# Twenty instead of twelve weight buffers for the streamed experts of a two-layer macaron block, eight of them filled when the expert stage begins

## The reference, cut to what matters

```python
# x: 2048 tokens x 256, E = 64 experts, M = 176, C = 96 slots for each expert, 6 experts for each token
slot = flat * C + jnp.minimum(pos, C - 1)
buf = jnp.zeros((E * C, H)).at[slot].set(x[tok]).reshape(E, C, H)
g = jnp.einsum('ech,emh->ecm', buf, Wg)
u = jnp.einsum('ech,emh->ecm', buf, Wu)
out = jnp.einsum('ecm,ehm->ech', silu(g) * u, Wd).reshape(E * C, H)
y = jnp.sum(out[slot].reshape(T, K, H) * topk_w[..., None], axis=1)
```

## Time and profile before

| | |
|---|---|
| median of 3 runs | 1694.56 us (1693.66 to 1703.97) |
| profiled execution, span from first to last instruction | 1695.7 us |
| busy: PE / DVE / ACT / POOL | 85% / 63% / 44% / 46% |
| DMA traffic in all | 145.50 MB |
| expert stage of layer 0 in the span | 123.1 to about 296 us |
| expert stage of layer 1 in the span | 785.0 to about 950 us |

### The profile page before, as it was taken

How to read it: one execution, slowest core, us unless ns; L and a number is a source line. 1 busy time by engine, 2 the same in 40 slices (tenths; PEclk the granted TensorE clock), 3 DMA queues, 4 the chain that set the end, 5 groups by cost and what they waited for, 6 DMA issues and landing times. The chain is left out here.

```text
span 1695.7 us, 39494 instructions
## 1 busy us (share of the span) xinstructions
PE 1441.4 (85%) x14334; PEld 990.9 (58%) x14334; DVE 1075.4 (63%) x2743; ACT 750.3 (44%) x1786; POOL 773.8 (46%) x741
## 2 busy tenths in 40 slices
PE   6879999448889996888999478877899999998799
PEld 3556656414545554455566356654677777777687
DVE  6852222457876564783222388876998888874888
ACT  5533333254555633553333311125776666752322
POOL 4453332763320000454333466606998888973000
PEclk9989999569999998899999788888999999999899
DMA  8309995631110002514999232200000000000000
GB/s 265 98 14 267 284 266 150 204 96 38 38 38 1 1 1 67 152 40 123 280 296 259 73 87 84 78 4 13 3 16 3 12 7 3 16 3 3 10 19 22
DMA packets 92664, 145.50 MB, mean 86 GB/s; under 512 B 25032, under 2 KB 52528, under 8 KB 92512
## 3 DMA queue, kind: packets, MB, share of 16 engines
q1 hardware_dynamic: 62816, 93.06, 19.1%
q0 software_dynamic: 15360, 37.77, 7.7%
q10 hardware_dynamic: 14336, 12.59, 2.7%
HBM read 122.39 MB, written 18.87 MB: 83 GB/s over the span
## 5 line engine op out<-in xcount | busy, mean ns | idle before, releaser
L2298 POOL TENSOR_TENSOR sb_m_prob<-sb_m_prob,sb_m_rinv 128x512 f32<-128x512 f32 x256 | 260.1, 1041 | 44.6 <-DVE sb_m_rinv L2348 40.8
L1272 POOL DMA_INDIRECT sb_c_rows<-slot_rows,sb_slot x192 | 192.1, 1000 | 102.7 <-issue 51.2
L2228 ACT ACTIVATE sb_m_prob<-m_ps_s,sb_m_nmax 128x512 f32<-128x512 f32 x256 | 173.8, 683 | 125.8 <-DVE sb_m_nmax L2354 125.2
L1106 POOL DMA_INDIRECT e_xn<-xn_rows,sb_table x128 | 117.7, 920 | 209.6 <-PE e_ps_x L1184 197.2
L1255 DVE TENSOR_TENSOR sb_e_h<-sb_e_sg,e_ps_gu 96x176 f32<-96x176 f32 x128 | 42.6, 333 | 256.5 <-ACT sb_e_sg L1231 256.5
L1193 PE MATMUL e_ps_gu<-e_wgu,sb_e_xT 128*96 128x352 f32 x512 | 178.1, 470 | 17.0 <-ACT sb_e_xT L1225 15.6
L2354 DVE TENSOR_REDUCE sb_m_nmax<-m_ps_s 128x1 f32<-128x512 f32 x256 | 163.8, 681 | 28.1 <-PE m_ps_s L2132 25.7
L2362 DVE STREAM_TRANSPOSE sb_m_pT<-sb_m_prob 128x1024 f32<-128x1024 f32 x128 | 157.5, 1232 | 0.0
L2145 PE MATMUL m_ps_v<-sb_m_pT,sb_m_lat_rows 32*64 32x128 f32 x8192 | 136.1, 275 | 4.6 <-issue 3.8
L2131 PE MATMUL m_ps_s<-sb_m_latT_high,sb_m_qa 128*128 128x512 f32 x256 | 125.5, 490 | 16.0 <-ACT sb_m_prob L2228 15.9
L2145 PEld LDWEIGHTS m_ps_v<-sb_m_pT,sb_m_lat_rows 32*64 32x64 f32 x8192 | 120.2, 131 | 27.8 <-issue 27.4
(11 more groups left out here) (280 smaller groups left out, 3076.4 us busy)
## 6 DMA issues: line engine op xcount, KB each, us to landing
e_wgu<-wgu SPq DMA_DIRECT2D x128, 352.0 KB, 4.9
e_wdn<-wdn SPq DMA_DIRECT2D x128, 192.0 KB, 4.7
slot_rows<-sb_e_y ACTq DMA_DIRECT2D x128, 96.0 KB
xn_rows<-e_xn SPq DMA_DIRECT2D x16, 256.0 KB, 2.2
sb_c_rows<-slot_rows,sb_slot POOLq DMA_INDIRECT x192, 2.8
sb_x<-x SPq DMA_DIRECT2D x4, 512.0 KB, 5.4
e_xn<-xn_rows,sb_table POOLq DMA_INDIRECT x128, 5.3
sb_g_zm<-wqT SPq DMA_DIRECT2D x1, 2048.0 KB, 9.1
```

The costliest lines, as they stand in the source:

```text
L1106: pool.indirect_dma_start(x, None, k.xn_rows[:, :], bass.IndirectOffsetOnAxis(ap=k.table[:, e:e + 1], axis=0))\
L1272: pool.indirect_dma_start(rows[u][j][:, :], None, k.slot_rows[:, :], bass.IndirectOffsetOnAxis(ap=k.slot[:, n, j:j + 1], axis=0))\
L2228: act.activation(prob[s % 4][:, hh, :], ps_s[j % 3][:, :], ACT.Exp, bias=nmax[s % 2][:, hh:hh + 1], accum_out=rsum[s % 2][:, hh:hh + 1]).t ...
L2298: pool.tensor_tensor(part, part, rinv[s % 2][:, hh:hh + 1].to_broadcast([P, T]), ALU.mult)\
```

## The change

`U` becomes 20. Eight more buffer pairs are allocated in the expert stage's own scope, where the SBUF of `route`'s own buffers is free again. As the stage's first work SP issues the 16 loads for experts 12 to 19, without a wait. Expert 20 and all later ones are loaded into the buffers of the expert 20 before. PE, ACT and DVE now have 20 steps written out, 2 rounds of 20 in the loop, and 7 left.

```diff
 AHEAD = 12
+MORE = 8
...
-    U, GA, LAG = AHEAD, 4, 3
+    U, GA, LAG = AHEAD + MORE, 4, 3
...
-        wgu, wdn = k.wgu, k.wdn
+        wgu = k.wgu + [sb(f"e{r}_more_wgu{u}", [P, DC, 2 * M0]) for u in range(MORE)]
+        wdn = k.wdn + [sb(f"e{r}_more_wdn{u}", [MH, 2, D]) for u in range(MORE)]
...
+            for u in range(AHEAD, U):
+                sp.dma_start(wgu[u][:, :, :], k.w["wgu0"][u]).then_inc(w_got[u], 16)
+                sp.dma_start(wdn[u][:, :, :], k.w["wdn0"][u]).then_inc(w_got[u], 16)
             with sp.Fori(1, E0 // U) as i:
                 for u in range(U):
                     load(i * U + u, u)
```

## The result

The changed kernel takes 1718.88 us (median, 1709.33 to 1720.69), against 1696.45 us of the kernel before on the same chip: a ratio of 1.0137, 95% interval 1.0098 to 1.0177. It is slower by 22 us where +12.5 us was forecast; 1718.88 lies in the range, 1.1 us from its upper end.

A forecast was written before the change was run, and what follows sets the result against it. Taken as bound: under full DMA engines, ScalarE's copy of y waiting for the store two experts before. Layer 0 +4.9 and layer 1 +7.6 give +12.5 us on the median 1694.6: 1707 us, range 1690 to 1720.

The forecast's parts named there:

- sum of bytes: Each expert stage: 28.97 MB of weights plus 0.197 MB per expert done, divided by the DMA rate, gives the loaded part's length.
- my own case: Expert stages: loaded pace 2.91 and 2.78 us per expert, +4.9 and +7.6 us; 1702 to 1712 us, chance 0.42.
- rival B: Expert stages: stores suffer, queued experts served early, ring of twenty binds, 46 experts done (the floor); 1716 us, chance 0.20.
- Edits at nothing: Expert stages: extra issues, written-out steps and gathers (0.9 + 6.6 us at worst, costing only over 9) add 0.
- n: Experts done when a stage's last weights land: 54 and 55 before, 48.4 and 49.2 forecast after.
- The pace behind the queue: Loaded part: 2.91 and 2.78 us per expert, between lower bounds 2.76 and 2.62 and upper bounds 3.06 and 2.94.
- A: Expert stages: a long queue treats stores as the short one does, pace unchanged; 1695 us, chance 0.27 together with no effect.
- C: Expert stages: engines work better always queued, stores hold their turn, PE keeps 2.38 us; 1665 us, chance 0.11.
- Step 1: Layer 0's stage start: 16 loads from 123.1, DMA full by 127, 270 to 300 GB/s already in 126 to 147.
- Step 2: First stretch: SiLU pace 2.8 to 3.1 us, not 2.36; copy of y's store waits over 70 us in total, not 57.5.
- Step 3: Layer 0's stage end: last load near 258 to 262, 46 to 49 experts done, tail of 15 to 18 at 2.3 us.
- Step 4: Expert stages: no wait for weights, before or after the change.

The follow-up runs named there:

- e5: The kernel before (ring of twelve) with four y buffers instead of two: 1669.52 us, ratio 0.9876.
- e7: The kernel before without the 52 loads of weights in each expert stage, experts 12 to 63 reusing the first twelve's weights: 1671.48 us, ratio 0.9870.
- e6: The changed kernel (ring of twenty) with four y buffers instead of two: 1675.93 us, ratio 0.9893.
- e10: The changed kernel with four y buffers, e6 run again on one chip beside other four-buffer schedules: 1675.24 us, ratio 0.9876.
- e8: The changed kernel's twenty buffers and loops, each load held until expert e - 8 is done (run-ahead of eight): 1695.80 us, ratio 0.9998.
- e1: The changed kernel's twenty buffers and loops, each load held until expert e - 12 is done, as before: 1696.33 us, ratio 0.9989.
- e3: e1 with run-ahead growing slowly from twelve to twenty, six loads per five experts done, no burst at the start: 1718.55 us, ratio 1.0129.
- e4: e1 with experts 12 to 19 loaded at once at the start, later loads held until expert e - 12 is done: 1703.00 us, ratio 1.0036.

## Why the prediction was right

The direction and the sum of bytes were right. That the time fell into the range is in part luck: it lies 1.1 us inside the upper end, outside the 1702 to 1712 of my own case, and the course of events was that of rival B.

**What bounds the kernel: right, and shown.** The copy of y waiting for the store two experts back sets the pace under load. Two more buffers bring 1.24% (e5), all that taking the loads away brings (e7), and with them the changed kernel's loss is gone (e6, e10).

**The deeper ring brings nothing directly: right.** Eight experts of run-ahead are as good as twelve (e8), twelve as good as before in the new code (e1).

**Edits at nothing: right for code, wrong for gathers.** e1 prices the code at nothing. The prediction let gathers take 0.9 + 6.6 us at worst; some took 8.3, and PE waited 2.25 us for the tokens of expert 4, which let it go 7.2 us after the issue. The sum had no such term: I had let it begin only above 9 us, counting on four full steps between issue and use. The first gathers of the stage don't have them: that one was issued at 126.5, and PE had nothing else to do from 131.4 on.

**The bytes: right in what they were used for.** Measured rates over the loaded parts were 279 and 278 GB/s; 278 and 288 were put in, so layer 1's was 3.5% too high, which is past the 3% that I had named as a sign of being wrong. Those windows hold the idle start. From the first transfer to the last landing that the trace gives, it is 283 and 282 GB/s, 2% off either way. n was forecast at 48.4 and 49.2, the floor at 46; it was 47 in both.

**The pace behind the queue: mis-sized, and of another shape.** This is the step that failed. I took the middle of two bounds, 2.91 and 2.78 us. The mean over the loaded part was 136.8/47 = 2.91 and 137.4/47 = 2.92. By the profile of before, layer 0's term was +5.9 for +4.9 and layer 1's +13.4 for +7.6, rival B's +13. By that of e1 they would be +11.0 and +7.5, so no more can be said than that the two together were +19.3 or +18.5 for +12.5. The shape was wrong in both layers: not one pace throughout but 4 us at first, beyond the upper bounds of 3.06 and 2.94, and then 2.6. That layer 0's mean is 2.91 to the digit is luck. The queue drained early, as rival B has it. A further 4 us of the profile lie outside the stages, in the scatter of that rest.

The upper bounds were too low because no stretch of the kernel before had a queue of that kind. Its loads landed in 4.9 us and its slowest store let a copy go after some 6.4. My own rule, that a step can't be shorter than half of landing and 0.5 us, gives (7.69 + 0.5)/2 = 4.1 us for the store above, which is the pace that was measured.

I had also tied the cost to the queue. e3 has the whole loss without a long queue and e4 a quarter of it with one, so most of the cost is that the loads run further ahead while stores are waited for: fewer experts are done in the loaded part, at a slower pace, and more are left for the tail.

**Rivals.** A (same pace, 1695) is out, as it took the queue of before for as good as a long one. Its stores were waited for up to 6.15 us in the rows shown, and 7.7 us is what the changed kernel has. The Trainium skill ("DMA: Bandwidth & Descriptors", section "Queues, rings and completion order") says that each DMA engine goes round its queues packet by packet. The change doesn't refute this: between e5 and e10 the loads' landing goes from 7.0 to 15.6 us and the stores' only from 6.3 to 6.9, which agrees with it nearly, while between e1 and e5 the stores' goes from 4.5 to 6.3 with loads at 5.0 and 7.0 (e5 also moves more, as its PE is faster). So it is the step from a short queue to a moderate one that delays a store, and I had priced the rule as if before had been beyond that step. B (1716) is nearest to what came: the queue served early, the ring of twenty binding, 47 done for its 46. C (1665, PE at 2.38 throughout) is out for this change, but 1670 us is what e5 reaches by the other road.

**Expectations on the changed profile.** Step 1 held two microseconds later (first load at 125.25, 272 GB/s from 126 to 147). Step 2 half: the first stretch was even slower than 2.8 to 3.1, yet the waits of the copy of y in layer 0 came to 45.1 us, not over 70; they were fewer and longer. Step 3 held: last load at 257.5 (258 to 262 was forecast), 47 experts begun, 17 in the tail. Step 4 held: no engine waits for weights.

**What the sum had wrong in its ground.** B = 278 GB/s was taken as the engines' limit, as their share read 1.03. e5 moved 310 GB/s at a share of 1.06. The rate under load was itself held down by PE's wait for the stores. The sum worked because it compared two kernels that both had this wait; it would have forbidden e5.

## What to carry to other kernels

Before giving a prefetch more depth, look for who waits for its data. Nobody did here, so more depth only brought the traffic forward, and what it delayed were the small transfers on which the pace hung. Look there instead: a store that must land before its buffer is used again wants as many buffers as its landing time under load spans steps (here 5 to 8 us over steps of 2.4: four, not two), and two more y buffers, 2 KB of each partition, brought 1.2% where eight more pairs of weight buffers, 38.9 KB of each partition, cost 1.4%. A busy share of 1.0 of the DMA engines is no proof that they can carry no more.

## What the runs showed of the hardware that was not expected

The DMA engines' busy share hardly tells their rate: 273 GB/s at 1.01, 281 at 1.05 in the changed kernel's first stretch, 294 at 1.02 in e3, 310 at 1.06 in e5, all with the same three kinds of transfers in somewhat different shares. What makes the difference stays open.

What a 96 KB store waits beside another queue's loads soon levels off. Median landings were 1.7 us alone (e7), 4.5 with loads that land in 5.0 (e1), 6.3 with loads at 7.0 (e5) and 6.9 with loads at 15.6 (e10). Single ones scatter widely: the longest that the changed kernel's gathers took behind the long queue was 8.4 us, and e1 has one of 8.0 without such a queue.

While PE was busy for 31.6 of 40 us, its granted clock had a mean of 0.83, and its 125 matmuls took 253 ns each; they take 198 ns each in e5 (103.00 us for 521, at 1.00). Over both stages PE's busy time grew by 4.8 us against before, with the same work. e3 has layer 0's loss at a clock of 0.99, so the lower clock comes on top and is not what the loss hangs on.
